# Two-layer graph convolution on one core: TensorE's signals sent by drains at the ends of its runs

## Chip, cores and metric

The kernel runs on one core of a Trainium2 chip. The metric is the device time of one execution in microseconds (us), without profiler, as the median of several runs. The engines are called TensorE (PE; PEld for its weight loads), VectorE (DVE), ScalarE (ACT), GpSimd (POOL) and SyncE (SP). Each has its own instruction stream, and they meet by semaphores: an instruction adds to one when it is done, and another engine waits until it has reached a value.

## What is computed

A graph of 50,000 nodes with 64 features each and 100,000 edges sorted by target (the last part of them are the nodes' edges to themselves) passes two layers; x is added at the end and each row is normalized:

```
def _ngcf_conv(x, W1, W2, src, dst, n_nodes):
    deg_out, deg_in = clipped counts of src and of dst
    norm = rsqrt(deg_out[src] * deg_in[dst])
    msg = (x[src] @ W1 + x[src] * x[dst] @ W2) * norm[:, None]
    return x @ W1 + segment_sum(msg, dst, n_nodes)
h = relu(_ngcf_conv(x, W1_1, W2_1, ...))
h = _ngcf_conv(h, W1_2, W2_2, ...)
out = layernorm(x + h)
```

Since x[dst] is the same for all edges of one target, the sum over edges of norm * x[src] is built first (s), and W1 and W2 are applied once a node: (x + s) @ W1 + (x * s) @ W2.

## The kernel before

A first part, `prepare`, sorts the edges without self loops into 394 chunks of 128, builds the rows' numbers, degrees and norms, and writes a table of rows to HBM. Then `layer` runs twice (l = 0 and 1), each time over the chunks in batches of 8 (48 full batches, then 4 + 4 + 2: 51 in all). Each batch b ends one group g of up to 8 tiles of 128 target nodes: 51 groups a layer.

The work of a step, by engine:

- **GpSimd** (`gpsimd`, L849) fetches each chunk's 128 source rows with one indirect gather, 8 a batch, into a ring of buffers (8 batches deep in layer 0, 3 in layer 1). Before chunks 0 and 4 of a batch it waits for `summed`, the signal that TensorE has used the old contents of that half.
- **VectorE** builds 0/1 selection tiles `sel` (L1141) and one-hot tiles for the count (L1185, L1188), splits the rows into three bf16 parts (L1163 to L1171, or L1151), joins a group's sums with its own rows (`join`, L1200, waits for `summed`), and makes u = s + x, v = s * x (`products`, L1235 and L1236; waits that an older group is turned). In layer 1 it also takes part in the row normalization.
- **TensorE** does, in `one_step(s)`, in this order: `multiply(g)` for the group before last (L908), `add_up(s)` (L882), `turn_over(g)` for the last group (L916), and in some steps `count(u)` (L893). `add_up` makes 96 bf16 matmuls of 128x64 (8 chunks, 4 tiles, 3 parts), signals `summed` after the first four chunks and after the last four. `turn_over` transposes 8 tiles of fp32 into PSUM and signals `turned`. `multiply` makes 8 fp32 matmuls of 128x64 (each stands as two in the trace) and signals `multiplied`. `count` makes 8 matmuls of 128x392 for a check of the degrees and signals `counted`; a layer has them in 2 (l = 0) or 5 (l = 1) of 6 steps of the loop. Steps 6 to 47 run in a hardware loop of 7 turns with 6 steps each.
- **ScalarE** copies the turned tiles back to SBUF (`turned_back`, L990, waits for `turned`), scales sums (L981) and own rows (L968), applies relu (L1001, L1004; waits for `multiplied`) or the squares and roots of layer 1, and writes y (L1009, L1029).
- **SyncE** stores y to the table of layer 1 or to the output.

The order on each engine is written out by hand. The signals of TensorE that the change touches all sat on the last matmul of a run:

```
if i == BATCH[b] - 1 or i % HALF_BATCH == HALF_BATCH - 1:
    last.then_inc(summed, 1)
```

The waits on TensorE are `until(uvt_made, ...)` before the products, `until(sel_made, ...)` and `until(split, ...)` before the sums, `until(uv_made, ...)` before the turns and before a group's first sum, and `until(hots_made, ...)` before the counts.

Of the kernel before, what the change touches and what calls it, by code (L numbers as in the profile page):

```python
# [7 lines left out]
P = 128  # L8
# [10 lines left out]
TILES = 392  # L19
# [14 lines left out]
def band(c):  # L34

    return range(max(0, (P * c - REACH) // CAP + 1), min(TILES - 1, (P * c + P - 1) // CAP) + 1)
# [584 lines left out]
GROUP = [(a, b + 1) for a, b in zip([0] + [t + 1 for t in LAST_TILE], LAST_TILE)]  # L621
# [3 lines left out]
BANKS = 3  # L625
# [9 lines left out]
COUNTS = [[COUNT_AT[l][s] for s in sorted(COUNT_AT[l])] for l in range(2)]  # L635
# [25 lines left out]
def ended(s):  # L661

    return [g for g in range(GROUPS) if ENDS[g] == s]
# [10 lines left out]
def layer(nc, l, x, out, tables, flag, keepers):  # L674

    k = keepers
    with ExitStack() as ctx:
        def sb(name, shape, dt=F32):
            return ctx.enter_context(nc.sbuf_tensor(f"c{l}_" + name, shape, dt))

        def sem(name):
            return k.stack.enter_context(nc.semaphore(f"c{l}_" + name))

        def ps(name, shape):
            return ctx.enter_context(nc.psum_tensor(f"c{l}_" + name, shape, F32))
# [3 lines left out]
        sel = sb("sel", [P, 2, 8, 4 * P], BF16)  # L689
        hot_l, hot_t, lane16 = sb("hot_l", [P, P, 8], F16), sb("hot_t", [P, 8, TILES], F16), sb("lane16", [P, CHUNKS], F16)  # L690
        own = sb("own", [P, 2, GN, D])
        uv, uvt = sb("uv", [P, 2, GN, 2, D]), sb("uvt", [P, 2, GN, P])
# [16 lines left out]
        else:  # L709
# [7 lines left out]
        p_sum = [ps(f"sum{i}", [P, GN, D]) for i in range(BANKS)]  # L717
        p_out = [ps(f"out{i}", [P, GN, D]) for i in range(2)]
        p_turn = [ps(f"turn{i}", [P, 4, P]) for i in range(2)]
        sel_made, summed, own_made, scaled_made, sums_made, uv_made, turned, uvt_made, multiplied = (sem(n) for n in (  # L720
            "sel_made", "summed", "own_made", "scaled_made", "sums_made", "uv_made", "turned", "uvt_made", "multiplied"))
        y_made, step_made, own_end_made = sem("y_made"), sem("step_made"), sem("own_end_made")
        hots_made, counted, lanes_read, split = sem("hots_made"), sem("counted"), sem("lanes_read"), sem("split")
# [23 lines left out]
        def parts(b):  # L747

            if l == 0:
                return tops(yr[:, b % 2]), tops(rest[:, b % 2]), lo[:, b % 2]  # L750
            first, left = first_and_rest(rows[:, b % RING])
            return first, halves(left)[:, :, :, 1], halves(left)[:, :, :, 0]
# [19 lines left out]
        def lanes_bank(b):  # L772

            bank = (p_out + p_turn + p_sum[2:])[b - AHEAD]
            return bank[:, :, :].rearrange("p a c -> p (a c)").bitcast(F16)
# [5 lines left out]
        def wide(g):  # L781
            return GROUP[g][1] - GROUP[g][0]
# [5 lines left out]
        def out_bank(g):  # L788

            return p_sum[(g - 1) % BANKS] if g in (g2, g3) else p_out[g % 2]  # L790

        def turn_bank(g, n):

            return p_turn[1 if g == g2 else n // 4]
# [57 lines left out]
        def tensor(pe):  # L852
            def turn_lanes(b):

                pe.wait_ge(k.lanes_hot, b + 1)
                for i in range(8):
                    last = nc.tensor.transpose(lanes_bank(b)[:, i * P:(i + 1) * P], lane_hot[b - AHEAD][:, :, i], k.ident16[:, :])
                last.then_inc(k.lanes_turned, 1)

            def meet(b, i):  # L860

                pe.wait_ge(k.lanes_back, b + 1)
                pe.wait_ge(k.degree_picked, 8 * b + i)
                nc.tensor.matmul(k.p_count[:, 0:TILES], lane_hot_t[b - AHEAD][:, i * P:(i + 1) * P], k.deg[:, :], start=True, stop=True).then_inc(k.degree_met, 1)

            def until(semaphore, first, turn, more):

                pe.wait_ge(semaphore, first if turn is None else turn * more + first)

            def add_up(b, turn=None):  # L870
                until(sel_made, b + 1, turn, STEPS_A_ROUND)
                until(split, b + 1, turn, STEPS_A_ROUND)
                for i in range(BATCH[b]):
                    c = FIRST[b] + i
                    for g in range(GROUPS):
                        if BEGINS[g] == c and g >= BANKS:
                            until(uv_made, g - BANKS + 1, turn, STEPS_A_ROUND)
                    for n, t in enumerate(band(c)):
                        g = GROUP_OF[t]
                        first = c == BEGINS[g] and t == GROUP[g][0]  # L880
                        for q, part in enumerate(parts(b)):
                            last = nc.tensor.matmul(p_sum[g % BANKS][:, t - GROUP[g][0], :], sel[:, b % 2, i, n * P:(n + 1) * P], part[:, i],  # L882
                                                    start=first and q == 0, stop=q == 2, skip_group_check=True)
                    if i == BATCH[b] - 1 or i % HALF_BATCH == HALF_BATCH - 1:
                        last.then_inc(summed, 1)
                    if b in LOOKUPS and i < 3:
                        meet(LOOKUPS[b], 5 + i)

            def count(u, turn=None):
                a, b = UNITS[u]  # L890
                until(hots_made, COUNTS[l].index(u) + 1, turn, len(COUNT_STEPS[l]))
                for i in range(b - a):
                    last = nc.tensor.matmul(k.p_count[:, 0:TILES], hot_l[:, :, i], hot_t[:, i], start=u == COUNTS[0][0] and i == 0,  # L893
                                            stop=True, skip_group_check=True)
                last.then_inc(counted, 1)

            def multiply(g, turn=None):
                until(uvt_made, g + 1, turn, STEPS_A_ROUND)
                if g in (g2, g3):
                    pe.wait_ge(uv_made, g)  # L900
                elif g >= 2:
                    until(y_made if l == 0 else centred, g - 1, turn, STEPS_A_ROUND)
                weights = k.wcat[:, l, :]
                if l == 1 and g in END_GROUPS:
                    pe.wait_ge(w_made, 1)
                    weights = w_centred[:, :]
                for n in range(wide(g)):
                    last = nc.tensor.matmul(out_bank(g)[:, n, :], uvt[:, g % 2, n, :], weights, start=True, stop=True)  # L908
                last.then_inc(multiplied, 1)

            def turn_over(g, turn=None):
                until(uv_made, g + 1, turn, STEPS_A_ROUND)
                if g:
                    until(uvt_made, g - 1 if g in (g2, g3) else g, turn, STEPS_A_ROUND)
                for n in range(wide(g)):
                    last = nc.tensor.transpose(turn_bank(g, n)[:, n % 4, :], uv[:, g % 2, n].rearrange("p a d -> p (a d)"), k.ident[:, :])  # L916
                last.then_inc(turned, 1)

            def tally():
                pe.wait_ge(tally_made, 1)  # L920
                nc.tensor.matmul(k.p_count[0:1, 400:404], k.ones[:, :], k.tally[:, :], start=True, stop=True).then_inc(tallied, 1)

            def one_step(s, turn=None):
                if s in LOOKUPS:
                    for i in range(5):
                        meet(LOOKUPS[s], i)
                if s == 1 and l == 0:
                    pe.wait_ge(k.lanes_back, EARLY)
                for g in ended(s - 2):
                    multiply(g, turn)  # L930
                add_up(s, turn)
                for g in ended(s - 1):
                    turn_over(g, turn)
                if s in COUNT_AT[l]:
                    count(COUNT_AT[l][s], turn)
            if l == 0:
                pe.wait_ge(k.lead_done, 1)
                pe.wait_ge(k.w_in, 64)
            for b in LOOKUPS.values():
                turn_lanes(b)  # L940
            for s in range(STEPS_A_ROUND):
                one_step(s)
            with pe.Fori(0, ROUNDS) as turn:
                for s in range(STEPS_A_ROUND, 2 * STEPS_A_ROUND):
                    one_step(s, turn)
            if l == 1:
                tally()
            add_up(b0)
            multiply(g0 - 1)
            turn_over(g0)  # L950
            add_up(b1)
            add_up(b2)
            turn_over(g1)
            multiply(g0)
            turn_over(g2)
            multiply(g1)
            turn_over(g3)
            multiply(g2)
            multiply(g3)
# [851 lines left out]
```

## Time and profile before

| | |
|---|---|
| median of 3 runs without profile | 1490.88 us (1488.17 to 1492.55) |
| profiled execution, span from first to last instruction | 1516.6 us |
| TensorE matmuls busy | 998.5 us, 66% |
| VectorE busy | 978.8 us, 65% |
| GpSimd busy | 795.9 us, 52% |
| ScalarE busy | 741.3 us, 49% |
| mean granted clock of TensorE | 0.757 |

The profiled execution has no time of its own beside its span here; the span is 25.7 us above the median of the runs without a profile. Times in the rows below are us from the span's start. Layer 0's first sums start at 155.8 us and its last at 799; layer 1's sums run from 821.2 to 1499.3. The end of a matmul in such a profile is modelled, its start is recorded. A wait whose releaser the profile can't name stands as "remote", one without any as "issue".

### The profile page before, as it was taken

What the parts mean: (1) busy time and instruction counts of PE and PEld (TensorE: products, weight loads), DVE (VectorE), ACT (ScalarE), POOL (GpSimd) and SP (SyncE); (2) the same over time, 40 slices, a digit from 0 to 9 for tenths busy, and PEclk for the clock granted to TensorE, in tenths of its full rate; (3) what the DMA queues carried; (4) which work ended last, traced back from release to release, by engine and by line L of the source; (5) the groups of instructions that cost most, each with busy time, mean ns of one, the idle gap of its engine ahead of it and who ended that gap; (6) DMA issues with size and microseconds to landing.
All of it is one profiled execution on the core that took longest, in us unless ns stands there. A gap on an engine that the chain in (4) does not pass through costs nothing. (4 is left out here: it accounts for less than half of the span.)

```text
span 1516.6 us, 33831 instructions
## 1 busy us (share of the span) xinstructions
PE 998.5 (66%) x13162; PEld 933.6 (62%) x13162; DVE 978.8 (65%) x2390; ACT 741.3 (49%) x2763; POOL 795.9 (52%) x813
## 2 busy tenths in 40 slices
PE   1775467666667666766783466767777667776676
PEld 1664356666666656766782366666666666666676
DVE  8577667565556655666583257767677767777676
ACT  3113145555555555655691145545554545555455
POOL 6575435555555555556205655655655555555540
PEclk9999567777777777667796667777787677777776
DMA  9854111122112211212112123333333233323322
GB/s 209 167 217 167 18 32 50 42 52 52 44 47 51 52 50 40 51 51 52 41 52 79 39 58 63 73 69 71 73 70 69 55 72 69 69 58 71 70 58 48
DMA packets 148693, 105.09 MB, mean 69 GB/s; under 512 B 115769, under 2 KB 128761, under 8 KB 147837
## 3 DMA queue, kind: packets, MB, share of 16 engines
q1 hardware_dynamic: 123176, 71.17, 17.8%
q0 software_dynamic: 25216, 32.50, 11.9%
q8 instruction: 33, 0.54, 0.1%
q10 hardware_dynamic: 212, 0.42, 0.1%
q14 instruction: 56, 0.45, 0.1%
HBM read 58.92 MB, written 45.11 MB: 69 GB/s over the span
## 5 line engine op out<-in xcount | busy, mean ns | idle before, releaser
L849 POOL DMA_INDIRECT c_rows<-table,k_row_i x394 | 380.3, 965 | 356.1 <-PE c_sum L882 159.7
L908 PE MATMUL c_out<-k_wcat,c_uvt 128*128 128x64 f32 x1516 | 319.6, 398 | 346.8 <-ACT c_uvt L990 309.5
L908 PEld LDWEIGHTS c_out<-k_wcat,c_uvt 128*128 128x128 f32 x1516 | 303.3, 306 | 373.3 <-ACT c_uvt L990 224.3
L849 POOL DMA_INDIRECT k_rows<-table,k_row_i x346 | 334.1, 966 | 294.5 <-PE c_sum L882 160.8
L990 ACT ACTIVATE c_uvt<-c_turn 128x512 f32<-128x512 f32 (+1 forms) x198 | 106.9, 590 | 539.2 <-remote 512.1
L1200 DVE TENSOR_TENSOR c_sum<-c_sum,c_own 128x512 f32<-128x512 f32 (+1 forms) x96 | 66.7, 695 | 381.9 <-remote 358.8
L882 PE MATMUL c_sum<-c_rows,c_sel 128*128 128x64 bf16 x4701 | 219.6, 221 | 48.2 <-issue 29.8
L882 PEld LDWEIGHTS c_sum<-c_rows,c_sel 128*128 128x128 bf16 x4701 | 219.3, 119 | 52.1 <-issue 50.3
L1141 DVE TENSOR_SCALAR c_sel<-k_place,k_grid 128x512 bf16<-128x512 f16 (+1 forms) x788 | 238.7, 371 | 0.0
L882 PE MATMUL c_sum<-c_yr,c_sel 128*128 128x64 bf16 x1567 | 209.6, 220 | 5.9 <-issue 4.4
L882 PE MATMUL c_sum<-c_rest,c_sel 128*128 128x64 bf16 x1567 | 207.8, 220 | 1.0 <-issue 1.0
L882 PE MATMUL c_sum<-c_lo,c_sel 128*128 128x64 bf16 x1567 | 207.0, 219 | 1.9 <-issue 1.8
L968 ACT ACTIVATE c_own<-k_xh 128x64 f32<-128x64 f32 x762 | 196.3, 399 | 0.0
L981 ACT ACTIVATE c_sum<-c_sum,k_xh 128x64 f32<-128x64 f32 x762 | 163.8, 318 | 62.4 <-DVE c_sum L1200 51.8
L882 PEld LDWEIGHTS c_sum<-c_yr,c_sel 128*128 128x128 bf16 x1567 | 183.4, 120 | 5.7 <-issue 4.2
L882 PEld LDWEIGHTS c_sum<-c_rest,c_sel 128*128 128x128 bf16 x1567 | 178.8, 117 | 5.6 <-issue 5.3
L882 PEld LDWEIGHTS c_sum<-c_lo,c_sel 128*128 128x128 bf16 x1567 | 177.3, 116 | 1.6 <-issue 1.6
L916 PE MATMUL c_turn<-k_ident,c_uv 128*128 128x128 f32 x784 | 109.3, 282 | 3.6 <-DVE c_uv L1236 3.3
L1188 DVE TENSOR_SCALAR c_hot_t<-k_place,k_grid 128x392 f16<-128x392 f16 x394 | 95.4, 314 | 0.0
L1029 ACT ACTIVATE c_y<-c_z,c_rstd 128x64 f32<-128x64 f32 x365 | 93.0, 372 | 0.3 <-DVE c_rstd L1281 0.3
L916 PEld LDWEIGHTS c_turn<-k_ident,c_uv 128*128 128x128 f32 x784 | 87.1, 145 | 4.2 <-DVE c_uv L1236 3.8
L1235 DVE TENSOR_TENSOR c_uv<-c_sum,k_xh 128x512 f32<-128x512 f32 (+3 forms) x102 | 67.7, 663 | 31.4 <-ACT c_sum L981 19.4
(210 smaller groups left out, 1231.6 us busy)
## 6 DMA issues: line engine op xcount, KB each, us to landing
table<-c_y SPq DMA_DIRECT2D x47, 384.0 KB
out<-c_y SPq DMA_DIRECT2D x47, 256.0 KB
c_res<-in_x SPq DMA_DIRECT2D x46, 256.0 KB
table<-k_xh SPq DMA_DIRECT2D x4, 1820.0 KB
c_rows<-table,k_row_i POOLq DMA_INDIRECT x394
k_rows<-table,k_row_i POOLq DMA_INDIRECT x346
table<-k_xh SPq DMA_DIRECT2D x1, 3575.0 KB
table<-k_xh SPq DMA_DIRECT2D x1, 1040.0 KB
```

What stands on the lines that cost most here:

```text
L849: nc.gpsimd.indirect_dma_start(out=rows[:, b % RING, i], out_offset=None, in_=tables[l], in_offset=bass.IndirectOffsetOnAxis(ap=k.row_i[:, ...
L882: last = nc.tensor.matmul(p_sum[g % BANKS][:, t - GROUP[g][0], :], sel[:, b % 2, i, n * P:(n + 1) * P], part[:, i], start=first and q == 0 ...
L908: last = nc.tensor.matmul(out_bank(g)[:, n, :], uvt[:, g % 2, n, :], weights, start=True, stop=True)
L916: last = nc.tensor.transpose(turn_bank(g, n)[:, n % 4, :], uv[:, g % 2, n].rearrange("p a d -> p (a d)"), k.ident[:, :])
L968: last = A(own[:, g % 2, t - a, :], k.xh[:, t, 0:D], ACT.Copy, scale=k.xh[:, t, D:ROW])
L981: last = A(p_sum[g % BANKS][:, t - a, :], p_sum[g % BANKS][:, t - a, :], ACT.Copy, scale=k.xh[:, t, D:ROW])
L990: last = A(uvt[:, g % 2, h:h + n, :], turn_bank(g, h)[:, 0:n, :], ACT.Copy)
L1029: last = A(y[:, g % 4, n, :], z[:, g % 4, n, :], ACT.Copy, scale=rstd[:, g % 4, n:n + 1])
L1141: last = V.tensor_scalar(sel[:, b % 2, i, 0:w], k.place[:, a:a + w], k.grid[:, 2, BACK + c:BACK + c + 1], None, ALU.is_equal)
L1188: last = V.tensor_scalar(hot_t[:, m], k.place[:, 0:TILES], k.grid[:, 0, slot], None, ALU.is_equal)
L1200: V.tensor_tensor(bank[:, 0:w], bank[:, 0:w], own_rows, ALU.add).then_inc(sums_made, 1)
L1235: V.tensor_tensor(uv[:, j, 0:w, 0, :], bank[:, 0:w], h, ALU.add)
```

## The change

In `add_up`, `count`, `multiply` and `turn_over`, the last matmul no longer carries the signal. A drain instruction of TensorE follows it and carries the signal instead; nothing else is changed. TensorE's other signals (`lanes_turned`, `degree_met`, `tallied`, and those of `prepare`) stay on their matmuls.

```
-                            last = nc.tensor.matmul(p_sum[g % BANKS][:, t - GROUP[g][0], :], sel[:, b % 2, i, n * P:(n + 1) * P], part[:, i],
+                            nc.tensor.matmul(p_sum[g % BANKS][:, t - GROUP[g][0], :], sel[:, b % 2, i, n * P:(n + 1) * P], part[:, i],
                                                     start=first and q == 0, stop=q == 2, skip_group_check=True)
                     if i == BATCH[b] - 1 or i % HALF_BATCH == HALF_BATCH - 1:
-                        last.then_inc(summed, 1)
+                        pe.drain().then_inc(summed, 1)
...
-                last.then_inc(counted, 1)
+                pe.drain().then_inc(counted, 1)
...
-                last.then_inc(multiplied, 1)
+                pe.drain().then_inc(multiplied, 1)
...
-                last.then_inc(turned, 1)
+                pe.drain().then_inc(turned, 1)
```

## Rows read from the trace of the kernel before

**Rows 1.** The core's span and mean granted clock; TensorE's line of the page.

```profile
core 0: 1516.6 us, clock 0.757
...
PE 998.5 (66%) x13162; PEld 933.6 (62%) x13162; DVE 978.8 (65%) x2390; ACT 741.3 (49%) x2763; POOL 795.9 (52%) x813
```

**Rows 2.** Waits: who waited for whom, us in total, times, longest us.

```profile
ACT c_uvt L990 <- remote: 512.1, 84, 9.2
DVE c_sum L1200 <- remote: 358.8, 83, 9.8
PE c_out L908 <- ACT c_uvt L990: 309.5, 77, 7.8
...
ACT k_xh L1001 <- PE c_out L908: 13.1, 20, 1.4
```

**Rows 3.** Timeline, TensorE, layer 1: start us, us, line, shapes, count, [idle before].

```profile
927.91 3.67 PE L908 MATMUL c_out<-k_wcat,c_uvt 128*128 128x64 f32 x16 [3.67 <-ACT c_uvt L990]
931.38 4.15 PE L882 MATMUL c_sum<-c_rows,c_sel 128*128 128x64 bf16 x96
935.37 1.07 PE L916 MATMUL c_turn<-k_ident,c_uv 128*128 128x128 f32 x8
936.27 1.49 PE L893 MATMUL k_p_count<-c_hot_t,c_hot_l 128*128 128x392 f16 x8
```

**Rows 4.** Timelines of ScalarE and of VectorE, same stretch.

```profile
926.70 1.09 ACT L990 ACTIVATE c_uvt<-c_turn 128x512 f32<-128x512 f32 x2 [6.41 <-remote]
...
940.34 1.08 ACT L990 ACTIVATE c_uvt<-c_turn 128x512 f32<-128x512 f32 x2 [6.45 <-remote]
...
940.32 0.70 DVE L1200 TENSOR_TENSOR c_sum<-c_sum,c_own 128x512 f32<-128x512 f32 x1 [3.15 <-remote]
```

**Rows 5.** Timeline of GpSimd, same stretch.

```profile
934.39 0.94 POOL L849 DMA_INDIRECT c_rows<-table,k_row_i  x1 [2.87 <-PE c_sum L882]
...
938.25 0.94 POOL L849 DMA_INDIRECT c_rows<-table,k_row_i  x1 [0.31 <-issue]
940.49 0.94 POOL L849 DMA_INDIRECT c_rows<-table,k_row_i  x1 [1.29 <-remote]
```

**Rows 6.** Timeline of TensorE and VectorE, layer 0, behind its last gather.

```profile
758.31 1.07 PE L916 MATMUL c_turn<-k_ident,c_uv 128*128 128x128 f32 x8
758.58 0.70 DVE L1200 TENSOR_TENSOR c_sum<-c_sum,c_own 128x512 f32<-128x512 f32 x1
```

**Rows 7.** Line L849: count, ns min/median/max, first and last start us.

```profile
L849 POOL DMA_INDIRECT c_rows<-table,k_row_i x394: 938/944/1472, 809.1 to 1488.1; - x197
L849 POOL DMA_INDIRECT k_rows<-table,k_row_i x346: 938/944/1722, 134.0 to 751.8; - x173
```

**Rows 8.** Timelines of TensorE's weight loads and of GpSimd, layer 1.

```profile
1111.15 1.78 PEld L882 LDWEIGHTS c_sum<-c_rows,c_sel 128*128 128x128 bf16 x33
1114.24 1.89 PEld L882 LDWEIGHTS c_sum<-c_rows,c_sel 128*128 128x128 bf16 x35 [1.31 <-issue]
...
1112.17 0.94 POOL L849 DMA_INDIRECT c_rows<-table,k_row_i  x1 [0.30 <-issue]
```

**Rows 9.** Line L1731 (ends of blocks), as rows 7; timeline of TensorE's last matmuls.

```profile
L1731 PEldq DRAIN  x2: 967/1818/2670, 803.6 to 1506.5; - x2
...
1505.87 3.25 PE L908 MATMUL c_sum<-c_w_centred,c_uvt 128*128 128x64 f32 x14
```

**Rows 10.** Window: us, busy (x) of PE, PEld, DVE, ACT, POOL, clock, DMA share, GB/s.

```profile
927.00:931.00 4.00, 3.08 (x15) 3.09 (x15) 3.65 (x12) 4.00 (x17) 3.09 (x4) 0.52 0.16 33
```

**Rows 11.** Timeline, TensorE, near the end of layer 1.

```profile
1502.55 1.11 PE L916 MATMUL c_turn<-k_ident,c_uv 128*128 128x128 f32 x4
```

**Rows 12.** Timelines of TensorE and of ScalarE, layer 0.

```profile
715.53 3.68 PE L908 MATMUL c_out<-k_wcat,c_uvt 128*128 128x64 f32 x16 [2.88 <-ACT c_uvt L990]
...
721.03 0.60 ACT L1001 ACTIVATE k_xh<-c_out 128x512 f32<-128x512 f32 x1 [2.03 <-remote]
```

**Rows 13.** Line L893, as rows 7.

```profile
L893 PE MATMUL k_p_count<-c_hot_t,c_hot_l x394: 326/329/387, 248.9 to 1476.5; 128*128 128x392 f16 x197
```

More of the change, by code:

```diff
@@ L892, in count @@
                 for i in range(b - a):
-                    last = nc.tensor.matmul(k.p_count[:, 0:TILES], hot_l[:, :, i], hot_t[:, i], start=u == COUNTS[0][0] and i == 0,
+                    nc.tensor.matmul(k.p_count[:, 0:TILES], hot_l[:, :, i], hot_t[:, i], start=u == COUNTS[0][0] and i == 0,
                                             stop=True, skip_group_check=True)
-                last.then_inc(counted, 1)
+                pe.drain().then_inc(counted, 1)
             def multiply(g, turn=None):
@@ L907, in multiply @@
                 for n in range(wide(g)):
-                    last = nc.tensor.matmul(out_bank(g)[:, n, :], uvt[:, g % 2, n, :], weights, start=True, stop=True)
-                last.then_inc(multiplied, 1)
+                    nc.tensor.matmul(out_bank(g)[:, n, :], uvt[:, g % 2, n, :], weights, start=True, stop=True)
+                pe.drain().then_inc(multiplied, 1)
             def turn_over(g, turn=None):
@@ L915, in turn_over @@
                 for n in range(wide(g)):
-                    last = nc.tensor.transpose(turn_bank(g, n)[:, n % 4, :], uv[:, g % 2, n].rearrange("p a d -> p (a d)"), k.ident[:, :])
-                last.then_inc(turned, 1)
+                    nc.tensor.transpose(turn_bank(g, n)[:, n % 4, :], uv[:, g % 2, n].rearrange("p a d -> p (a d)"), k.ident[:, :])
+                pe.drain().then_inc(turned, 1)
             def tally():
```

## The prediction

> **What bounds the kernel now.** I read the page first, then the waits, then timelines of one engine each. The page shows no full engine: TensorE is busy 66% of a span of 1516.6 us, and its granted clock moves between half and full [rows 1]. The waits say who is late. ScalarE waits 512.1 us in 84 turns for something "remote" before it copies the turned tiles (L990), VectorE waits 358.8 us before it joins the sums (L1200), and TensorE waits 309.5 us for ScalarE's copy [rows 2]. All three belong to one ring that goes round once a step: TensorE turns a group, ScalarE copies it, TensorE multiplies it and adds up the next batch.
>
> One step of layer 1 shows where the ring stands still. TensorE's product begins at 927.91, the sums at 931.38, the turns end at 935.37 + 1.07 = 936.44, the counts at 937.76 [rows 3]. Yet ScalarE begins its copy, which needs only the turns, at 940.34, and VectorE its join, which needs only the sums, at 940.32 [rows 4]. Both signals are 3 to 5 us late, and they come together. ScalarE's copy one step earlier began at 926.70, so a step is 13.64 us, of which TensorE works 9.8.
>
> What ends the hold is seen on GpSimd: four gathers from 934.39 to 938.25 + 0.94 = 939.19, then, 1.13 us behind their end, the two signals (940.32), and the next gather at 940.49 [rows 5]. Where no gather runs (layer 0's last started at 751.8) the turns end at 758.31 + 1.07 = 759.38 and VectorE's join starts at 758.58, while TensorE is still turning [rows 6, 7]. So TensorE's signals are held while gathers are in flight. Nor is it only the signal: behind the product at 1111.15 TensorE issued 33 weight loads without a pause, then stood for 1.31 us for "issue" and went on at 1114.24, 1.13 us after the gather of 1112.17 ended [rows 8]. I read this as TensorE's instructions not retiring while gathers are in flight, so that its queue fills.
>
> The Trainium skill ("SBUF — State Buffer", section "SBUF: two separate sides") says that only the port pair of VectorE and GpSimd is shared and that TensorE never waits on anyone. By that rule the gathers could not hold TensorE and a step would be some 11 us. The rows disagree, and I follow them.
>
> **The change, part by part.** Each of the five kinds of run (first half and second half of the sums, turns, counts, products) loses the signal of its last matmul and gets a drain, on which TensorE's sequencer stands until all older instructions are complete. About 500 drains are added. What was queued behind the signal at once (weight loads of the next run) now waits. The trace has two drains of TensorE, at the blocks' ends. The later began at 1506.5 and took 2.670, so it ended at 1509.17, while the last matmul ended at 1505.87 + 3.25 = 1509.12 [rows 9]: a drain itself is 0.05 us. No gather ran there, so how it behaves in the hold isn't shown; that is the disputed cost.
>
> The Trainium skill ("PSUM — Partial Sum Buffer", section "Engine vs sequencer instructions") says that a drain waits for the engine to go fully idle, and that the signal belongs on the matmul. Taken with the stall above this speaks against the change; the sum below doesn't use it.
>
> My forecast: the drain is held just as the signal was. Then per step, from the moment R at which the sums' signal comes:
> 1. R itself stays. The first half's signal starts the four gathers (GpSimd had been idle), which end 4.80 us later, plus 1.13. The drain adds 0.05 to it.
> 2. The turns used to be done inside the hold. Now they stand behind the second half's drain, and start at R. Eight at full clock take 1.07 [rows 3]. After some 4 us of standing the granted clock is near its low level of 1.2 GHz: in the product that follows today's idle it is 0.52 of full [rows 10]. Four turns near the end took 1.11 [rows 11]; a further one is (1.11 - 0.42)/3 = 0.23, so eight take 2.0. With issue and drain 2.15. Bounds 1.2 and 2.15.
> 3. The turns' drain may be held by the gathers that R has started. Bounds: 0, and the whole second group (5.93 us from R, so 3.4 more). Nearest row: the product's signal, which today falls in the same group. In layer 0 a product ended at 715.53 + 3.68 = 719.21 and ScalarE took it at 721.03, 1.82 late; over all, ScalarE waited 13.1 us in 20 of 51 products (0.26 each), and "remote" waits add a little [rows 2, 12]. I take 0.4.
> 4. The counts' drain keeps the product back. The eight counts take 1.49 at full clock [rows 3], and ScalarE's copy gives 927.91 - 926.70 = 1.21 of cover, so 0.6 with the drain's own bubble; at half clock the spacing of (1.49 - 0.33)/7 = 0.166 doubles, and it is some 1.7. The counts are 394/8 = 49 runs in 102 groups [rows 13]: 0.3 to 0.8 a step, I take 0.6.
> 5. The product's drain stops the weight loads of the sums, which now start 3.47 after the product's start, inside its last matmul. A matmul of 0.42 and the drain, issue and load again: 0.5. It too may be held: 0.4 as in 3 (0 to 1.3).
> 6. The first half's drain leaves a bubble of 0.3, but what follows it (second half, 1.5 to 2.5 us) lies under the four gathers: nothing. If that cover were gone it would cost 0.3.
>
> Sum: 0.05 + 2.15 + 0.4 + 0.6 + 0.9 = 4.1 us a step. The steps with gathers are (346 + 394)/8 = 92, from the count of L849's instructions [rows 7]. 92 x 4.1 = 377 us. The span shown would be 1516.6 + 377 = 1894; it is 26 us above the median of the runs without profile, to which I add the same: 1491 + 377 = **1868 us**. All low ends (1.2 + 0 + 0.3 + 0.5) give 2.0, or 1675; all high ends (5.6 + 0.8 + 1.8 with 0.05) give 8.2, or 2250, which needs each step to meet the worst hold. The case's own range is 1680 to 2150. What is late next is the same ring, with more of it in series; GpSimd, at eight gathers of 1.25 us, has more slack than before.
>
> **The rivals.**
> - *The drain gets round the hold.* Only the matmul's own signal is held, the matmuls are done, and a sequencer's signal goes out at once. For it: signals that are freed come together (940.32, 940.34), though the matmuls that they belong to end 1 us apart [rows 3, 4]. Against: the stall of TensorE itself [rows 8]. Then a step is 1.21 (copy) + 3.47 + 0.5 (product) + 3.99 + 0.6 (sums) + 1.07 + 0.1 (turns) + 0.3 (counts) = 11.2 in place of 13.64. GpSimd's floor, 8 x 1.25 + 0.5, lies below. 92 x 2.4 = 221 less: 1270 us.
> - *The drain completes, but its signal is held.* TensorE goes on, R and the turns' signal come together as now, and what is left is the product's bubble before the first half's signal, 0.5 + 0.05: 92 x 0.55 = 51 more, 1542 us. For it: in the steady step TensorE's work goes on through the gathers, product, sums and turns [rows 3, 5]; against: again the stall. It has the forecast's sign and an eighth of its size.
> - *Nothing to tell.* Part of the hold goes (fewer instructions in flight when a signal is due) and pays the bubbles of 0.55 a step just so: within 0.3% of 1491, which would be chance.
>
> **How the numbers follow.** Chances: held drain 0.50, signal held alone 0.15, round the hold 0.27, nothing 0.08. The predicted time is that of the first. The point from which the second rival decides is whether a drain of the second half ends before or after GpSimd's fourth gather. Leaving out the lower half of the fast case (0.13) and the top of the slow one (0.06), the range is 1268 to 2060; the likeliest case's own is 1680 to 2150. A measurement of this kernel tells 0.3% from nothing (the three runs lie within 0.3%). Faster 0.28 (the fast case and a little of the balance), same 0.05, slower 0.67.
>
> **What would show it.** In the changed profile: drains of TensorE of 3 to 5 us behind the second half; turns that begin at the time of VectorE's join and not 4 us before it; the "remote" wait of ScalarE before L990 longer than 512 us; a step of 17 to 18 us; mean clock below 0.757 [rows 1]. Wrong, if drains are all under 0.6 us; if then ScalarE's copy starts within 0.2 us of the turns' end, the fast rival holds, and if it starts with the join, the middle one.

## The result, and the profile after

The changed kernel took 1739.27 us (median of 4 runs, 1734.63 to 1756.8) beside 1491.72 us (1488.17 to 1493.79): a ratio of 1.167, 95% interval 1.161 to 1.173. The forecast was 1868 us, with a range of 1268 to 2060. The sign and the mechanism came out as forecast; the loss is 248 us where 377 were expected. Some executions of a kernel take over 1.5% longer than its fastest; the ratios below leave those out.

The profile after, first what answers to [rows 1]: the span and mean granted clock, and the busy time of each engine (the profiled execution took 1738.99 us, close to the median, while the profiled span of the kernel before lies 25 us above that kernel's median; so the spans differ by 221 us and the medians by 248).

```profile
core 0: 1737.3 us, clock 0.719
```

```profile
PE 1105.8 (64%) x13162; PEld 945.0 (54%) x13162; DVE 987.7 (57%) x2390; ACT 743.0 (43%) x2763; POOL 796.5 (46%) x813
```

Its waits, as [rows 2] (who for whom, us in total, times, longest):

```profile
ACT c_uvt L990 <- PEq L917: 690.5, 90, 12.7
DVE c_sum L1200 <- PEq L885: 479.7, 89, 17.3
...
PE c_turn L916 <- issue: 313.7, 101, 4.6
...
ACT k_xh L1001 <- PEq L909: 39.4, 37, 5.0
...
PE c_out L908 <- ACT c_uvt L990: 34.2, 29, 1.3
```

"Remote" has a name now: PEq L885 and L917, the drains of TensorE's sequencer. TensorE hardly waits for ScalarE's copy any more (34.2 us, was 309.5 in [rows 2]). It stands for 313.7 us ahead of the turns instead, for "issue", which is the drain.

One step of layer 1, TensorE's timeline (start us, us, line, shapes, count, [idle before]). It answers to [rows 3].

```profile
1107.51 4.87 PE L882 MATMUL c_sum<-c_rows,c_sel 128*128 128x64 bf16 x96 [0.32 <-issue]
1116.40 1.94 PE L916 MATMUL c_turn<-k_ident,c_uv 128*128 128x128 f32 x8 [4.02 <-issue]
1118.55 2.83 PE L893 MATMUL k_p_count<-c_hot_t,c_hot_l 128*128 128x392 f16 x8 [0.21 <-issue]
1121.61 1.99 PE L908 MATMUL c_out<-k_wcat,c_uvt 128*128 128x64 f32 x16 [0.23 <-issue]
1123.93 3.24 PE L882 MATMUL c_sum<-c_rows,c_sel 128*128 128x64 bf16 x96 [0.33 <-issue]
```

The same stretch on VectorE (the join), ScalarE (the copy) and GpSimd (the gathers), as [rows 4, 5]:

```profile
1116.29 0.70 DVE L1200 TENSOR_TENSOR c_sum<-c_sum,c_own 128x512 f32<-128x512 f32 x1 [6.25 <-PEq L885]
...
1118.39 1.09 ACT L990 ACTIVATE c_uvt<-c_turn 128x512 f32<-128x512 f32 x2 [12.16 <-PEq L917]
...
1110.52 0.94 POOL L849 DMA_INDIRECT c_rows<-table,k_row_i  x1 [8.58 <-PEq L885]
...
1114.26 0.95 POOL L849 DMA_INDIRECT c_rows<-table,k_row_i  x1 [0.31 <-issue]
1116.46 0.95 POOL L849 DMA_INDIRECT c_rows<-table,k_row_i  x1 [1.25 <-PEq L885]
```

And its drains, one window each (duration ns min/median/max, first and last start us): the first half's, the second half's, the turns', the product's.

```profile
L885 PEldq DRAIN  x1: 1148/1148/1148, 1109.1 to 1109.1; - x1
L885 PEldq DRAIN  x1: 4482/4482/4482, 1111.7 to 1111.7; - x1
L917 PEldq DRAIN  x1: 1943/1943/1943, 1116.4 to 1116.4; - x1
L909 PEldq DRAIN  x1: 1940/1940/1940, 1121.7 to 1121.7; - x1
```

The sums end at 1107.51 + 4.87 = 1112.38, the drain behind them at 1111.7 + 4.48 = 1116.2, the join starts at 1116.29, and only then, at 1116.40, do the turns. In [rows 3, 4] the turns were over almost 4 us before the join. The fourth gather ends at 1115.21, the drain some 1.0 us later. The turns' drain, though the second group of gathers is running, ends with the turns: the copy starts at 1118.39, and the turns end at 1118.34.

Means over the 88 steps with eight turns between 200 and 1700 us, worked out from the starts and ends on the timelines:

```
us per step                        before   after   difference
sums' start to VectorE's join        8.51    7.75     -0.76
join to ScalarE's copy               0.46    1.91     +1.45
copy                                 1.09    1.09      0
copy's end to product's start        0.08    1.29     +1.21
product                              3.42    2.98     -0.44
product's end to next sums' start   -0.20    0.66     +0.86
step                                13.35   15.69     +2.34
```

A negative time from the product's end to the next sums' start means that they overlap. 92 steps of 2.34 are 215 us of the 221 between the two spans.

### The profile page after: what moved, and what is told of

Its sections match the earlier page's. It is cut to its first block and busy times, and to the rows that moved or that the text cites. A ratio compares the mean times of both kernels' runs of the same rounds, so it can differ in the third digit from the quotient of the medians.

```text
span 1737.3 us, 34283 instructions
## 1 busy us (share of the span) xinstructions
PE 1105.8 (64%) x13162; PEld 945.0 (54%) x13162; DVE 987.7 (57%) x2390; ACT 743.0 (43%) x2763; POOL 796.5 (46%) x813
## 3 DMA queue, kind: packets, MB, share of 16 engines
q0 software_dynamic: 25216, 32.50, 10.2%
## 5 line engine op out<-in xcount | busy, mean ns | idle before, releaser
L849 POOL DMA_INDIRECT c_rows<-table,k_row_i x394 | 383.3, 973 | 460.7 <-PEq L885 293.4
L849 POOL DMA_INDIRECT k_rows<-table,k_row_i x346 | 332.0, 959 | 409.0 <-PEq L885 318.3
L990 ACT ACTIVATE c_uvt<-c_turn 128x512 f32<-128x512 f32 (+1 forms) x198 | 107.0, 591 | 740.6 <-PEq L917 690.5
L916 PE MATMUL c_turn<-k_ident,c_uv 128*128 128x128 f32 x784 | 162.5, 375 | 314.4 <-issue 313.7
L908 PEld LDWEIGHTS c_out<-k_wcat,c_uvt 128*128 128x128 f32 x1516 | 269.3, 275 | 125.8 <-issue 94.6
L908 PE MATMUL c_out<-k_wcat,c_uvt 128*128 128x64 f32 x1516 | 283.5, 365 | 83.2 <-issue 48.8
L916 PEld LDWEIGHTS c_turn<-k_ident,c_uv 128*128 128x128 f32 x784 | 129.4, 194 | 324.4 <-issue 323.2
L882 PE MATMUL c_sum<-c_rows,c_sel 128*128 128x64 bf16 x4701 | 207.6, 215 | 90.4 <-issue 70.7
L882 PEld LDWEIGHTS c_sum<-c_rows,c_sel 128*128 128x128 bf16 x4701 | 195.2, 113 | 104.8 <-issue 104.6
L882 PE MATMUL c_sum<-c_rest,c_sel 128*128 128x64 bf16 x1567 | 216.9, 222 | 0.0
L882 PE MATMUL c_sum<-c_lo,c_sel 128*128 128x64 bf16 x1567 | 216.3, 222 | 0.0
L893 PE MATMUL k_p_count<-c_hot_t,c_hot_l 128*128 128x392 f16 x394 | 123.3, 483 | 18.9 <-issue 18.8
L893 PEld LDWEIGHTS k_p_count<-c_hot_t,c_hot_l 128*128 128x128 f16 x394 | 57.7, 160 | 73.4 <-issue 66.1
```

Of the source, the lines that this page charges most:

```text
L849: nc.gpsimd.indirect_dma_start(out=rows[:, b % RING, i], out_offset=None, in_=tables[l], in_offset=bass.IndirectOffsetOnAxis(ap=k.row_i[:, ...
L990: last = A(uvt[:, g % 2, h:h + n, :], turn_bank(g, h)[:, 0:n, :], ACT.Copy)
```

## The experiments

Ratios are to the kernel before, timed on the same chip in the same set.

**1. Which drain.** Only the second half's drain (`second_only`), or all others (`all_but_second`):

```
-                        last.then_inc(summed, 1)
+                        (pe.drain() if i == BATCH[b] - 1 else last).then_inc(summed, 1)
```

> Kernel before, with a drain only behind the second half of each batch's sums (99 drains of the 500). Theory 1 (one drain matters: TensorE stands on it until about 1 us behind the fourth gather, so the turns and counts that used to be done in that time come after it): nearly the whole loss, +2.1 to +2.7 us in each of 92 steps, 1685 to 1740 us. Theory 2 (each drain costs its own bubble of some 0.5 us, 248 us over 500 drains, wherever it stands): +50 us, about 1540 us.

> The changed kernel, but the second half's signal is back on its last matmul; the other 400 drains stay. Theory 1: the turns lie in the waiting time again; what is left are the counts behind the turns' drain (0.3 to 0.6 us a step) and the product's bubble (0.3 to 0.5): 1545 to 1590 us. Theory 2: 400 drains of 0.5 us, about 1690 us.

Measured: 1610.88 us, ratio 1.065 (1.059 to 1.072), and 1634.69 us, ratio 1.077 (1.069 to 1.085). Neither theory's numbers hold. The second half's drain alone gives well under half of the loss, not nearly all, and the others more than my 55 to 100 us, but nothing like 200. In `all_but_second` the hold moved on to the turns' drain, late in 87 of 88 cases (table in experiment 6). In `second_only` the drain is held in the same way. L885 has now the second halves' drains alone (ns min/median/max):

```profile
L885 PEldq DRAIN  x102: 553/4646/5903, 160.8 to 1591.5; - x102
```

Worked out as in the table above, the join-to-copy time grew here by the same 1.46 us, and the copy-to-product time by 0.47. But the product, which now follows work and not a long idle, fell from 3.42 to 2.76 us, and the time from the sums' start to the join by 0.37. That gave back 1.0 us a step; the step grew by 0.92.

**2. The same without gathers.** Each gather becomes a plain copy of 128 consecutive rows, so the rows are the wrong ones. Once with signals on the matmuls (`plain_signal`), once with the drains (`plain_drain`):

```
-                    nc.gpsimd.indirect_dma_start(out=rows[:, b % RING, i], ...)
+                    c = min(c, TILES - 1)
+                    nc.gpsimd.dma_start(out=rows[:, b % RING, i], in_=tables[l][c * P:(c + 1) * P, :])
```

> Kernel before, with each indirect gather replaced by a plain copy of 128 consecutive rows of the table, issued by GpSimd (the rows are then the wrong ones; bytes, buffers and semaphores are the same). Theory 1 takes it that the gathers hold TensorE's instructions: without them signals come at once, a step is about 11.2 us, and the time 1260 to 1330 us. If it is the bytes moved and not the gather instruction, or another thing, that holds them, the time stays near 1490 us.

> The changed kernel with the same plain copies in place of the gathers (the rows are the wrong ones). Theory 1: no drain is held, so what the drains cost here is their bubbles alone, 0.3 to 0.9 us a step over the kernel with plain copies and no drains: a ratio of 1.02 to 1.06 between the two. Theory 2: the whole 250 us again, a ratio of about 1.18 to 1.2.

Measured: 1051.34 us, ratio 0.694 (0.690 to 0.698), and 1115.43 us, ratio 0.738 (0.733 to 0.742). The drains cost 64 us here, 1.061 times, or 0.14 us each (the trace has 452, not 500). VectorE is near its limit here (below), so part of the drains' price may be hidden. If the 64 us are their own price, they are a quarter of the 248 us, and three quarters come with the gathers. The page of `plain_signal`, its busy times and GpSimd's queue (packets, MB, share):

```profile
PE 791.6 (75%) x13162; PEld 729.0 (69%) x13162; DVE 947.4 (90%) x2390; ACT 741.3 (71%) x2763; POOL 485.7 (46%) x813
...
q0 software_dynamic: 25216, 32.50, 12.9%
```

The queue and its 25216 packets are those of the kernel before. TensorE's and GpSimd's timeline in it:

```profile
625.70 2.98 PE L882 MATMUL c_sum<-c_rows,c_sel 128*128 128x64 bf16 x96
...
635.84 4.47 POOL L850 DMA_DIRECT2D c_rows<-table  x8 [4.06 <-PE c_sum L882]
```

VectorE is 90% busy, and TensorE's 96 matmuls take 2.98 us instead of 4.15 [rows 3]. With plain copies no drain behind sums took longer than 1.15 us (`plain_drain`, L885); with gathers the median of those behind a second half was 4.65 (above). The copy differs from the gather in its instruction and in the order of the rows that it reads, and no run tells the two apart.

```profile
L885 PEldq DRAIN  x198: 552/702/1150, 150.1 to 1095.1; - x198
```

**3. One kind at a time.** The same edit at the turns (`turned_only`), the products (`product_only`), the first halves (`first_only`), each alone:

```
-                last.then_inc(turned, 1)
+                pe.drain().then_inc(turned, 1)
```

> Kernel before, with a drain only behind the turns (102 drains). The first set showed the loss split: second half's drain alone 1.065, all others 1.077. Theory 3: the turns' drain stands in the hold that the first gathers make, so the counts of half the steps start after it, beside ScalarE's copy of 1.2 us: 1.2 to 1.6 us more in half the steps, less what the product gains from a warmer clock: 40 to 65 us, ratio 1.03 to 1.045. Theory 2 (a drain's own bubble, 64 us for 500 drains by the run without gathers): 13 us, ratio 1.01.

> Kernel before, with a drain only behind the products (102 drains). Theory 3: it is held in about four steps of ten, behind the second group of gathers, and keeps the next sums back: 0.3 to 0.9 us a step, 30 to 80 us, ratio 1.02 to 1.055. Theory 2: 13 us, ratio 1.01.

> Kernel before, with a drain only behind the first half of each batch's sums (96 drains). The prediction's step 6 (no gather runs there, and the 0.3 us bubble lies under the four gathers that follow): ratio 1.00 to 1.005. Rival (the signal of the first half is itself on the path, since the gathers that it starts end the hold; a drain that comes later by the rest of the pipeline moves that end): 0.05 to 0.3 us a step, ratio 1.005 to 1.02. If it were more, the part of the loss that second half, turns and products leave open would lie here.

Measured: turns 1536.39 us, ratio 1.014 (1.007 to 1.022); products 1568.55 us, 1.036 (1.030 to 1.041); first halves 1494.22 us, 1.001 (0.996 to 1.005). The product's drain is theory 3's. The turns' ratio lies between the theories, nearer to a bare bubble, though the trace shows theory 3's mechanism (timelines of TensorE and ScalarE):

```profile
1017.53 1.07 PE L916 MATMUL c_turn<-k_ident,c_uv 128*128 128x128 f32 x8
1022.42 2.05 PE L893 MATMUL k_p_count<-c_hot_t,c_hot_l 128*128 128x392 f16 x8 [3.82 <-issue]
1024.26 3.52 PE L908 MATMUL c_out<-k_wcat,c_uvt 128*128 128x64 f32 x16
...
1022.26 1.09 ACT L990 ACTIVATE c_uvt<-c_turn 128x512 f32<-128x512 f32 x2 [6.52 <-PEq L917]
```

The drain of these turns, in a window of its own:

```profile
L917 PEldq DRAIN  x1: 4600/4600/4600, 1017.6 to 1017.6; - x1
```

The counts wait for it and start beside the copy, so the product starts 0.9 us behind the copy's end (1.18 in the mean of the steps with counts, was 0.08). It is paid in half of the steps and partly won back. First halves cost nothing, as step 6 of the prediction had it.

The four single ratios, each with an interval of 0.4 to 0.8% to either side, multiply to 1.065 x 1.014 x 1.036 x 1.001 = 1.120, and 1.167 / 1.120 = 1.042 is left for the counts' drain, which was not run alone, and for what the drains do together. One such joint effect is read from the traces: in the steps with counts the copy-to-product time is 1.18 us in `turned_only` and 2.22 in the changed kernel, 1.04 x 50 steps = 52 us, or 3.4% of 1517 (this set's kernel before).

**4. Signal or stop.** All signals stay on matmuls; a drain without one follows the second half:

```
                         last.then_inc(summed, 1)
+                    if i == BATCH[b] - 1:
+                        pe.drain()
```

> Kernel before, its signals all on the matmuls, and one drain without a signal behind the second half of each batch's sums. Theory 1 (the loss is that TensorE stands and the turns come late): the same as with the signal on that drain, ratio 1.055 to 1.075. Rival (a signal sent by a drain is what arrives late, the standing costs nothing): ratio 1.00 to 1.01.

Measured: 1605.66 us, median of 4 (1578.34 to 1608.07), beside 1486.75. By the rule for ratios its fastest run is left to compare: 1578.34 us, 1.062 times the kernel before, without an interval. It lies close to `second_only`'s 1.065 and far above the rival's 1.01. So the loss is TensorE's standing, not the way in which the signal is sent.

**5. Where the gathers start.** GpSimd waits for the whole batch before all 8 gathers, without drains (`late_signal`) and with them (`late_drain`):

```
-                    if i % HALF_BATCH == 0:
-                        done(pool, summed, sums_of(b - RING) - 1 + i // HALF_BATCH)
+                    if i == 0:
+                        done(pool, summed, sums_of(b - RING))
```

> Kernel before, no drain, but GpSimd waits for the second half of the sums before all 8 gathers of a batch (it used to start 4 of them at the first half). Theory 4 (signals are late because gathers start while the sums run): the sums' signal now finds no gather, the turns' signal comes within 2 us of the first gather's start, where it was prompt behind the drains: a step of 10.5 to 11.5 us, 1250 to 1330 us. Rival (every signal of TensorE waits until a running train of gathers ends): the turns' signal comes behind the eighth gather, 11.4 us after the sums', and a step is about 20 us: over 2000 us.

> The changed kernel (all drains) with the same late start of all 8 gathers. Theory 4: the second half's drain ends at once, the turns' too; the counts' and the product's may be held to the end of the eight gathers: a step of 11.5 to 14 us, 1330 to 1550 us, and not above the changed kernel. Rival: about 20 us a step, over 2000 us.

Measured: 1614.47 us, ratio 1.065 (1.059 to 1.071), and 1704.46 us, ratio 1.126 (1.119 to 1.133). Theory 4 was right on the signals and wrong on the time. The join starts 0.11 us behind the sums' end and the copy 0.04 behind the turns' end (medians in `late_signal`; 4.4 and 3.7 in the kernel before). But the hold comes back later in the train of gathers (gathers that follow each other without a wait between them): in `late_signal` as TensorE's own starts.

```profile
1111.53 1.85 PE L916 MATMUL c_turn<-k_ident,c_uv 128*128 128x128 f32 x8
1113.22 1.49 PE L893 MATMUL k_p_count<-c_hot_t,c_hot_l 128*128 128x392 f16 x8
1114.56 2.00 PE L908 MATMUL c_out<-k_wcat,c_uvt 128*128 128x64 f32 x16
1116.39 0.87 PE L882 MATMUL c_sum<-c_rows,c_sel 128*128 128x64 bf16 x24
1117.66 0.22 PE L882 MATMUL c_sum<-c_rows,c_sel 128*128 128x64 bf16 x2 [0.40 <-issue]
1119.10 0.19 PE L882 MATMUL c_sum<-c_rows,c_sel 128*128 128x64 bf16 x1 [1.22 <-issue]
...
1123.37 3.63 PE L882 MATMUL c_sum<-c_rows,c_sel 128*128 128x64 bf16 x66 [1.20 <-issue]
...
1111.83 0.70 DVE L1200 TENSOR_TENSOR c_sum<-c_sum,c_own 128x512 f32<-128x512 f32 x1 [3.87 <-PE c_sum L882]
...
1113.42 1.09 ACT L990 ACTIVATE c_uvt<-c_turn 128x512 f32<-128x512 f32 x2 [8.72 <-PE c_turn L916]
...
1111.99 0.94 POOL L849 DMA_INDIRECT c_rows<-table,k_row_i  x1 [5.25 <-PE c_sum L882]
...
1121.22 0.95 POOL L849 DMA_INDIRECT c_rows<-table,k_row_i  x1 [0.30 <-issue]
```

The turns end at 1113.38, and the copy starts 0.04 us later in the middle of the train. The sums, which need nothing that is missing, get six matmuls into 5.7 us from 1117.66 on and run again from 1123.37, 1.2 us behind the eighth gather's end (1122.17). Here the wait that the late gathers took away is paid by the next sums.

**6. How many matmuls.** The first of the two signals of sums moves from the fourth to the seventh chunk, with drains (`seventh_drain`) and without (`seventh_signal`):

```
-                    if i == BATCH[b] - 1 or i % HALF_BATCH == HALF_BATCH - 1:
+                    if i == BATCH[b] - 1 or BATCH[b] == 8 and i == 6:
```

> The changed kernel, but the first of a batch's two signals of sums comes behind the seventh chunk and not the fourth: GpSimd's gathers then start some 0.3 us behind it, with 12 matmuls of the sums left and not 48. Theory 5 (a count: in the runs so far TensorE's signal was prompt where up to some 16 matmuls had been started since the first gather of a train, and late from about 20 on): the second drain ends within 0.1 us of its matmul, the turns' drain in most steps too, the product's is held to the end of the eight gathers: a step of 14 to 15 us, ratio to the kernel before 1.05 to 1.12. Theory 6 (a matter of kind: sums are held, turns and counts are not): the second drain is held to 1 us behind the fourth gather as in the changed kernel, ratio 1.14 or more.

> Kernel before, no drain, with the same shift of the first signal. Theory 5: the second signal of the sums is prompt (VectorE's join within 0.1 us of the last matmul), the turns' signal too; the product's signal and the next sums are held: as the late start of all gathers, less about 1 us a step: ratio 0.98 to 1.04. Theory 6: the sums' signal is held from the first gather's start, about 1 us before their end, to 1 us behind the fourth gather: the join 5 us late, ratio 1.06 to 1.15.

Measured: 1661.18 us, ratio 1.118 (1.108 to 1.128), and 1559.32 us, ratio 1.049 (1.040 to 1.058), the first inside theory 5's range, the second just past the upper end of it, and both below theory 6's. In `seventh_signal`, which has no drains, the join starts 0.11 us behind the sums' end in the median, where it was 4.4: the signal is prompt too. Timelines of TensorE and GpSimd in `seventh_drain`:

```profile
1103.40 5.24 PE L882 MATMUL c_sum<-c_rows,c_sel 128*128 128x64 bf16 x96 [6.18 <-issue]
1108.88 1.06 PE L916 MATMUL c_turn<-k_ident,c_uv 128*128 128x128 f32 x8 [0.23 <-issue]
1110.16 1.54 PE L893 MATMUL k_p_count<-c_hot_t,c_hot_l 128*128 128x392 f16 x8 [0.21 <-issue]
1111.93 1.97 PE L908 MATMUL c_out<-k_wcat,c_uvt 128*128 128x64 f32 x16 [0.23 <-issue]
...
1108.34 0.95 POOL L849 DMA_INDIRECT c_rows<-table,k_row_i  x1 [6.98 <-PEq L885]
...
1117.10 0.95 POOL L849 DMA_INDIRECT c_rows<-table,k_row_i  x1 [0.30 <-issue]
```

Its second half's drain and its product's, of the same step:

```profile
L885 PEldq DRAIN  x1: 483/483/483, 1108.2 to 1108.2; - x1
...
L909 PEldq DRAIN  x1: 7732/7732/7732, 1112.0 to 1112.0; - x1
```

The second half's drain takes 0.48 us where it took 4.48, with the same kind of matmul in front of it and the first gather running. So kind alone doesn't decide. Nor does time alone. Below are drains against the matmuls of TensorE started since the first gather of a train (gathers less than 0.6 us apart), worked out from the traces; "late" is over 0.3 us behind the last matmul's modelled end.

```
kernel           drain behind   matmuls since   us since    late
seventh_drain    second half      4 to 7          0.3       0 of 91
changed kernel   turns            4 to 11         1.9       0 of 60
changed kernel   counts          12 to 19         5.0       0 of 27
seventh_drain    counts          20 to 23         3.5       0 of 47
product_only     product         16 to 19         4.1      43 of 70
late_drain       product         20 to 23         4.9      33 of 34
seventh_drain    product         28 to 31         4.8      34 of 35
second_only      second half     32 to 39         1.1 to 1.9  89 of 89
changed kernel   second half     40 to 43         1.8      84 of 91
turned_only      turns           40 to 47         2.1      86 of 88
all_but_second   turns           48 to 51         2.8      87 of 88
changed kernel   turns           48 to 51         5.3       7 of 23
changed kernel   counts          56 to 59         7.9      13 of 16
```

Few matmuls: prompt, even 3.5 us into a train that goes on for 6 more (the counts in `seventh_drain`). Thirty and more: mostly late, even 1.1 us into it. The turns show it for one kind at nearly one time: 0 of 60 late about 1.9 us into the train with 4 to 11 matmuls, 86 of 88 at 2.1 us with 40 to 47. Between 16 and 23 the products are mostly late (76 of 104) and the counts never (0 of 47). Those counts stood only 8 matmuls behind the last drain, the products 16 and more, so kind and distance from the last drain are not told apart there. In the last two lines the two groups of gathers follow each other without a gap. The turns, 8 matmuls behind a held drain that has just ended, are mostly prompt, but the counts, again 8 matmuls behind a drain, are mostly late. So the number counts, but it isn't the whole rule. What in the gather does this stays open.

None of these kernels beats the one before with its gathers in place.

## Why the prediction was right, and where its sizes were off

The forecast was that the drain is held just as the signal was, and that the turns then stand behind it. The changed profile shows it as stated there: drains of 4 to 5 us behind the second half, turns that begin with the join, ScalarE's wait up from 512 to 690.5 us, the clock down from 0.757 to 0.719. The rule it was set against is that TensorE never waits on anyone (the Trainium skill, "SBUF — State Buffer", section "SBUF: two separate sides"). The page says so of SBUF's ports. Taken as the prediction took it, that no gather can hold TensorE back, it fails here by experiment too: with plain copies for the gathers the time falls by 30%, and no drain behind sums takes over 1.15 us. Whether the hold arises at a port of SBUF no run shows. The step grew to 15.7 us, not 17 to 18. Term by term:

- **Step 1, "R itself stays", +0.05:** measured -0.76 from the sums' start to the join, the largest miss. In the kernel before, the second group of gathers often still runs when the sums start, and they stall as in [rows 8] (in 70 of the 88 steps a train, or the 1.1 us behind it, still runs at the sums' start; in the changed kernel in 5). The first halves take 2.87 us in the mean before and 2.48 after; the rest of the way to the join shrinks by 0.4 more. The trace shows where; no run tested it by itself.
- **Steps 2 and 3, turns behind R and their drain, 2.15 + 0.4:** measured +1.45. The turns took 1.67 in the mean, not 2.0, the copy was already 0.46 behind the join before (I had set it at 0), and the turns' drain was late in 7 of 102 cases, 11.2 us in all: 0.11 a step, since mostly few matmuls stand between it and the second group's first gather (experiment 6). The upper bound of step 3 is a slip: by its own numbers it is 5.93 - 2.15 = 3.8, not 3.4. It moves only the high end.
- **Step 4, counts, 0.6:** measured +1.21. In the steps that have them the product starts 2.22 us behind the copy's end: they run at half clock, behind the drains of second half and turns both (2.83 us in the step above, 1.49 in [rows 3]). Their own drain, for which the sum had no hold, was late in 13 of 50 cases, 22.9 us in all or some 0.26 a step.
- **Step 5, product's drain, 0.9:** measured +0.86. Here it was held in 10 of 102 cases, 29.8 us in all or some 0.34 a step, beside the 0.4 assumed. Alone it costs 3.6%.
- **Left out of the sum, the clock given back, 0.44 a step.** The old product ran after a long idle at half clock; now turns and counts run just ahead of it. Two products of the changed kernel (windows: first and last us, us, busy of PE, PEld, DVE, ACT, POOL, clock, DMA share, GB/s), the first behind 1.5 us of idle and the second straight behind eight counts:

```profile
1103.50:1107.20 3.70, 3.65 (x16) 3.49 (x16) 3.31 (x11) 2.73 (x12) 0.00 (x0) 0.50 0.00 0
1121.60:1123.60 2.00, 1.99 (x16) 1.86 (x16) 1.77 (x3) 2.00 (x10) 0.00 (x0) 0.99 0.10 25
```

- **Step 6, first half, nothing:** ratio 1.001 (0.996 to 1.005).

So the sum was 4.1 and the measured step +2.34: the terms added to the ring were about right in total (3.5 against 4.1), and two gifts of the new order, 1.2 us, were not looked for. The forecast also took it that the median lies 26 us below the span after the change too; it lies 2 us above it. In spans the miss is 377 against 221, in medians 377 against 248.

Of the rivals, "the drain gets round the hold" (1270 us) and "it completes, but its signal is held" (1542 us) are both excluded by the second half's drain, which ended 1.0 us behind the fourth gather and held the turns until 1116.40; both rivals have it end with its matmul. `bare_second` speaks against the second too.

## What to carry to other kernels

In these runs a drain released nothing earlier than the last matmul's signal had; it only stopped TensorE from working ahead of it, so its price is the work that used to lie inside the wait for that signal. Before putting one in, ask of each place whether such a wait exists there: here it cost 0.14 us without gathers (beside a VectorE that was 90% busy), nothing behind first halves, and 6.5% of the kernel behind second halves. When a ring of waits gets new serial terms, look also for what idle time they fill, because the clock and the neighbour's slack give part of it back.

## What was not expected of the hardware

- The gathers of GpSimd cost this kernel more than any edit of its order did: 1051 us with plain copies of as many bytes and packets against 1517 with gathers in the same set. GpSimd's own instructions take 0.56 us each instead of 0.97, but the ring waited for TensorE's held signals, not for GpSimd.
- While a train of gathers runs TensorE may not only signal late but start late: one matmul per 0.7 to 1.4 us, until 1.2 us behind the last gather.
- A drain that isn't held ends 0.02 us behind the last matmul's modelled end in the median of each kind (1 late of the 455 in `plain_drain`), and the next run starts 0.2 to 0.3 us later.
